# Two changes to an attention loop: the bursts of score products change places, and GpSimd takes over two small steps on the row maxima

## What is computed

```python
Q, K, V = heads(x @ Wq.T + bq), heads(x @ Wk.T + bk), heads(x @ Wv.T + bv)   # 32 query, 8 key/value heads of 16
Q, K = rope(Q, K)
w = softmax(Q @ K.T / 4)                        # per head 1024 x 1024, no mask
x = layernorm(x + (w @ V) @ Wo.T + bo)
x = layernorm(x + ffn(x))                       # silu(x Wg) * (x Wu) Wd, inner size 1408
```

## Time and profile before

| what | value |
|---|---|
| median of 3 runs | 1063.87 us (1063.75 to 1064.66) |
| profiled execution, its own time | 1064.13 us |
| its span, first to last instruction | 1062.3 us |
| PE busy | 97% |
| DVE busy | 76% |
| ACT busy | 63% |
| POOL busy | 25% |
| granted TensorE clock, mean | 0.998 of full speed |

### The profile page before, as it was taken

One profiled execution on the slowest core, in us unless ns is written; L12 is line 12 of the kernel. 1 busy time (PEld: TensorE's weight loads), 2 busy tenths in 40 slices (PEclk: granted clock), 3 DMA queues, 4 the chain that ended last, 5 costly groups with the idle time before them and its releaser, 6 DMA issues.

```text
span 1062.3 us, 15699 instructions
## 1 busy us (share of the span) xinstructions
PE 1026.5 (97%) x5858; PEld 536.8 (51%) x5858; DVE 809.5 (76%) x1199; ACT 665.1 (63%) x1346; POOL 266.2 (25%) x227
## 2 busy tenths in 40 slices
PE   8999999999999999999999999999999999999996
PEld 3643344433443433443444443333337888888885
DVE  4899978899779799779988899999803475662535
ACT  2368877788778788778766678888863431222221
POOL 2751030141335422246200042844100000000002
PEclk9999999999999999999999999999999999999999
DMA  5274417243142512344140446531217510402011
GB/s 200 80 196 126 106 35 213 52 97 78 52 115 75 105 56 54 82 108 105 34 78 12 116 120 150 124 121 37 93 68 193 166 40 9 111 28 52 1 39 42
DMA packets 64432, 94.87 MB, mean 89 GB/s; under 512 B 37536, under 2 KB 37920, under 8 KB 62272
## 3 DMA queue, kind: packets, MB, share of 16 engines
q1 hardware_dynamic: 63776, 93.10, 33.2%
q10 hardware_dynamic: 576, 0.72, 0.2%
HBM read 53.95 MB, written 27.00 MB: 76 GB/s over the span
## 4 chain that ended last, share of the span: by engine, by line
PE 80%; DVE 10%; ACT 6%; issue 2%; DMA 1%; SPq 0%; POOL 0%; DVEq 0%; POOLq 0%
PE PS L448 21%; PE PV L467 20%; PE PSA L537 15%; PE PS L554 5%; PE PSA L426 5%; DVE nmx L964 5%; PE PS L365 4%; ACT Bn L756 3%; PE PS L493 2%; PE PSA L493 2%; DVE nmx L960 2%; DVE nmx L957 2%; ACT Bn L765 2%; PE PV L554 2%; PE PSA L365 1%
## 5 line engine op out<-in xcount | busy, mean ns | idle before, releaser
L756 ACT ACTIVATE Bn<-PS 128x512 f32<-128x512 f32 x1146 | 548.8, 559 | 125.0 <-PE PS L448 111.1
L448 PE MATMUL PS<-Qt,Kt 50*128 50x512 f32 x1146 | 391.7, 434 | 20.0 <-ACT Bn L756 18.7
L426 PE MATMUL PSA<-Kt,Qt 48*128 48x512 f32 x1024 | 390.0, 459 | 2.2 <-DVE Kt L936 0.8
L964 DVE TENSOR_REDUCE nmx<-PSA 128x1 f32<-128x1024 f32 x256 | 312.2, 1219 | 61.0 <-PE PSA L426 59.8
L448 PEld LDWEIGHTS PS<-Qt,Kt 50*128 50x128 f32 x1146 | 184.4, 184 | 323.6 <-ACT Bn L756 312.7
L467 PE MATMUL PV<-Bn 128*32 128x512 f32 x2048 | 272.8, 605 | 0.0
L426 PEld LDWEIGHTS PSA<-Kt,Qt 48*128 48x128 f32 x1024 | 174.6, 183 | 21.7 <-DVE nmx L964 6.2
L960 DVE TENSOR_REDUCE nmx<-PSA 128x1 f32<-128x512 f32 x256 | 174.5, 682 | 1.4 <-PE PSA L426 1.1
L957 DVE TENSOR_REDUCE nmx<-PSA 128x1 f32<-128x512 f32 x256 | 174.3, 681 | 0.0
L537 PE MATMUL PSA<-x1Th,wr 128*128 128x512 f32 x344 | 135.0, 393 | 0.8 <-DVE sg L1052 0.5
L537 PE MATMUL PSA<-x1Tl,wr 128*128 128x512 f32 x344 | 134.7, 392 | 0.0
(11 more groups left out here) (166 smaller groups left out, 919.4 us busy)
## 6 DMA issues: line engine op xcount, KB each, us to landing
Qt<-pscr SPq DMA_DIRECT2D x90, 128.0 KB, 4.9
A<-in_wf SPq DMA_DIRECT2D x11, 768.0 KB, 6.3
wr<-A SPq DMA_DIRECT2D x33, 256.0 KB, 2.9
pscr<-A SPq DMA_DIRECT2D x16, 512.0 KB, 3.7
vscr<-Bn SPq DMA_DIRECT2D x32, 256.0 KB, 2.0
Kt<-pscr SPq DMA_DIRECT2D x90, 64.0 KB, 2.3
A<-A SPq DMA_DIRECT2D x16, 256.0 KB, 3.7
Bn<-vscr SPq DMA_DIRECT2D x8, 512.0 KB
```

The lines of the kernel that those rows point to most:

```text
L426: op = e.matmul(PSA[:, 2 * s + h, :], Qt[n % 3][p:p + NC_, g % 2, 128 * qt:128 * qt + 128], Kt[n % 3][p:p + NC_, 512 * h:512 * h + 512], s ...
L448: e.matmul(PS2[:, i, cols], Kt[n % 3][rows, 128 * kt:128 * kt + 128], Qt[n % 3][rows, g % 2, 512 * qh + cols.start:512 * qh + cols.stop], ...
L756: e.activation(Pb[c % NP_][:, cols], PS2[:, score_bank[c, p], cols], ACT.Exp, scale=0.25).then_inc(*act_exp.next(piece(c, p)))
L964: e.tensor_reduce(nmx[:, hh % 2, c0:c0 + 1], slot_pair(s), AX.XY, ALU.max, negate=True).then_inc(*dve_max[s].next(k))
```

## The change

- The weighing comes behind the fourth score tile in even units and behind the third in odd ones, so that the bursts of three and five change places; the tile in two pieces is now the one with c % 8 == 7, again the first behind the burst of three.
- Background work on PE stands right behind the weighing as before, which is now between the third and the fourth tile of the unit. ACT evacuates a projection there, and DVE does its adds and norms between the two parts of the unit's second step.
- For the half rows 1 to 30, DVE only joins the maxima in the unit with u % 8 == 3; POOL rounds and takes the rest; DVE transposes one unit later, behind its second step.
- SP calls `write_max` in the units with u % 8 == 4 (for the last half row in unit 243), still ahead of all else in that unit.
- Three steps of the rotation of the second projection come one unit later.

```diff
-                    (0, 4): (1, "rope"), (0, 7): (1, "h0"), (0, 9): (1, "h1"), (0, 10): (1, "out")}
+                    (0, 4): (1, "rope"), (0, 8): (1, "h0"), (0, 10): (1, "h1"), (0, 11): (1, "out")}
...
+        def apart(hh):
+            return 1 <= hh < 2 * NG - 1
+        def low_max(hh):
+            return (pool_ms if apart(hh) else dve_ms).at(("low", hh))
...
-            return [slice(0, 128), slice(128, 512)] if c % 8 == 3 and c < 4 * SPLIT else [slice(0, 512)]
+            return [slice(0, 128), slice(128, 512)] if c % 8 == 7 and c < 4 * SPLIT else [slice(0, 512)]
...
-            last = score_bank[4 * u + 3, len(pieces(4 * u + 3)) - 1]
+            last = score_bank[4 * u + 2, 0]
...
 # PE
-                    if u >= 1 and g == (2, 3)[u % 2]:
+                    if u >= 1 and g == (3, 2)[u % 2]:
                         weigh(u - 1)
+                        background(u)
...
 # ACT
                     exponent(u, g)
+                    if g == 2 and at_u in project_at:
+                        for h, i in enumerate(free_banks(u)):
+                            evacuate_raw(project_at[at_u], h, i)
...
 # DVE
-                if k % 16 == 15:
-                    turn_max(hh)
+                if 1 in halves and k % 16 == 15:
+                    join_max(hh)
+                    if not apart(hh):
+                        split_max(hh)
+                        turn_max(hh)
+                if 1 in halves and k % 16 == 1 and k > 16 and apart(k // 16 - 1):
+                    turn_max(k // 16 - 1)
...
+                k = next(steps)
+                if at_u in norm_at or at_u in out_at or at_u == values_at:
+                    maximum(k, (0,))
...
+                    maximum(k, (1,))
...
 # POOL
+            def split_max(hh):
+                top = nmx[:, hh % 2, 0:16]
+                w.wait_ge(*dve_ms.at(("join", hh)))
+                w.wait_ge(*dve_ms.at(("turn", hh - 1)))
+                e.tensor_copy(msp[:, 0:16], top).then_inc(*pool_ms.next(("high", hh)))
+                w.wait_ge(*pool_ms.at(("high", hh)))
+                e.tensor_tensor(msp[:, 16:32], top, msp[:, 0:16].bitcast(F32), ALU.subtract).then_inc(
+                    *pool_ms.next(("low", hh)))
...
+                if u % 8 == 3 and apart(steps_done(u) // 16 - 1):
+                    split_max(steps_done(u) // 16 - 1)
                 if at_u in project_at:
                     rope(project_at[at_u])
...
 # SP
-                if steps_done(u) // 16 > steps_done(u - 1) // 16:
+                if u % 8 == 4:
                     write_max(steps_done(u) // 16 - 1)
+                if u == SPLIT - 1:
+                    write_max(2 * NG - 1)
```

More of the change, by code:

```diff
@@ L251, in post_ln_layer @@
         dve_out, dve_turn, dve_parts = count("dve_out"), count("dve_turn"), count("dve_parts")
+        pool_ms = count("pool_ms")
         pool_one, pool_cs, pool_rope = count("pool_one"), count("pool_cs"), count("pool_rope")
@@ L665, in tensor, with background @@
                     project_half(1, 1, 3, ((0, 1), (2, 3))[k - 2])
+            def background(u):
+                at_u, pair = divmod(u, 16), free_banks(u)
+                if at_u in project_at:
+                    for h, i in enumerate(pair):
+                        project_half(project_at[at_u], h, i, (0, 1, 2, 3))
+                if at_u == values_at:
+                    for t in range(8):
+                        value_rows(1, t, pair[t // 4])
+                if at_u in out_at:
+                    t2 = out_at[at_u]
+                    out_project(False, 0, t2, [bank(i) for i in pair], [bank_free[i] for i in pair])
+                    for j, i in enumerate(pair):
+                        bank_free[i] = dve_y.at((False, 0, 2 * t2 + j))
             for u in range(SPLIT):
@@ L894, in scalar @@
                     exponent(u, g)
+                    if g == 2 and at_u in project_at:
+                        for h, i in enumerate(free_banks(u)):
+                            evacuate_raw(project_at[at_u], h, i)
                 if u >= 1:
                     finish(u - 1)
-                if at_u in project_at:
-                    for h, i in enumerate(free_banks(u)):
-                        evacuate_raw(project_at[at_u], h, i)
                 if at_u in rope_end and rope_end[at_u][1] in ("h0", "h1"):
@@ L945, in add_values, with maximum @@
                     ALU.add).then_inc(*dve_val.next((b, h)))
-            def maximum(k):
+            def maximum(k, halves=(0, 1)):
                 if k >= len(stream):
@@ L953, in maximum @@
                 if hh >= 2:
-                    w.wait_ge(*dve_ms.at(("low", hh - 2)))
+                    w.wait_ge(*low_max(hh - 2))
                 if by_halves(k):
[L956 to L961, removed]
+                    for h in halves:
+                        w.wait_ge(*pe_max.at((k, 0) if h == 0 else k))
+                        col = nmx[:, hh % 2, c0 + 16 * (h == 0):c0 + 16 * (h == 0) + 1]
+                        e.tensor_reduce(col, slot_pair(s)[:, h, :], AX.X, ALU.max, negate=True).then_inc(
+                            *dve_max[s].next((k, 0) if h == 0 else k))
                 else:
@@ L965, in maximum, with join_max @@
                         *dve_max[s].next(k))
-                if k % 16 == 15:
-                    turn_max(hh)
-            def turn_max(hh):
+                if 1 in halves and k % 16 == 15:
[5 more added lines that the diff above has]
+                    turn_max(k // 16 - 1)
+            def join_max(hh):
                 top, rest = nmx[:, hh % 2, 0:16], nmx[:, hh % 2, 16:24]
@@ L980, in turn_max @@
                     *dve_ms.next(("low", hh)))
-                w.wait_ge(*dve_ms.at(("low", hh)))
+            def turn_max(hh):
+                w.wait_ge(*low_max(hh))
                 if hh >= 2:
@@ L1218, in vector @@
                 maximum(next(steps))
[L1219 to L1226, removed]
+                k = next(steps)
+                if at_u in norm_at or at_u in out_at or at_u == values_at:
+                    maximum(k, (0,))
+                    if at_u in norm_at:
+                        first_norm(False, 0, norm_at[at_u])
+                    if at_u == values_at:
+                        for h, i in enumerate(free_banks(u)):
+                            add_values(1, h, i)
+                    if at_u in out_at:
+                        add_rows(False, 0, out_at[at_u], [bank(i) for i in free_banks(u)])
+                    maximum(k, (1,))
+                else:
+                    maximum(k)
                 if at_u in recip_at:
```

## The result

| | before | after |
|---|---|---|
| median of the runs | 1063.81 us | 1125.66 us (1123.25 to 1129.66, 4 runs) |
| ratio | | 1.0586, 95% interval 1.0574 to 1.0598 |
| profiled execution, its span | 1064.13, 1062.3 us | 1126.11, 1124.3 us |
| granted TensorE clock, mean | 0.998 | 0.962 |

The change makes the kernel 5.9% slower. Slower is what was forecast, but 1126 lies 7 us above the end of the range (1119).

What follows compares the result with a forecast made beforehand. The prediction took a ring of PE, ACT and DVE with little slack to bound the kernel. Its sum was 1064.1 - 19.2 (gains) + 60.7 (SP's order) + 2 (clock) = 1107.6 us, 1107 against the median; range 1078 to 1119.

Steps and rivals of the forecast that it cites:

- The copy (13.3): ACT's copy of PV moves behind the burst of five into idle time: 0.46 saved in 29 half rows, 13.3 us.
- the turn (5.9): Turn of the maxima split between DVE and POOL: PE's 0.44 stall goes in 14 half rows, 5.9 us gained.
- Background work and rounding at 0: Moved projection work on PE and ACT's rounding steps of the rotation: costs only change places, 0 us.
- The cover that I named for the rope: On POOL the rope waits behind the split, but its swap lands later anyway: 0 us.
- SP's order, 60.7: write_max on SP falls behind what u % 8 == 3 issues, so maxima land late at ten places: 60.7 us lost.
- t0: Start of PE's short piece in the unit with u % 8 == 3, from which SP's delays are counted.
- The two guesses at 512 KB and 768 KB in front: At (4,3) and (12,3) the gather runs behind big reads: 2.9 and 4.9 us lost.
- The clock, 2: PE's clock may fall behind the stalls; taken as 2 us, since most of a pair waits for ACT.
- The upper bound, 25: Clock term's upper bound: a pair at twice its time behind each of five stalls over 5 us, 25 us.
- The reciprocal's read does hold the write: Rival denied this: only gathers hold the maxima's write, (8,3) loses 8.2, losses 37.3, total 1082 us; chance 0.18.
- Small writes do not pass the big transfers: Rival said they pass: only SP's time to issue counts, 16.1 us lost, total 1061 us; chance 0.10.
- The gains did not fail: Rival said copy or POOL comes late each half row while stalls stay: up to 19 more, 1126 us; chance 0.06.

Runs made afterwards that it cites:

- the runs of each part alone: Kernel after with only the bursts, or only POOL's split of the turn, SP's order mended in both (the division moved too for the split): 1057.91 and 1061.37 us.
- the bursts alone: Kernel after with the whole turn back on DVE and SP's mended order (swap first, write_max ahead of reciprocal, parts and gather): 1057.91 us, ratio 0.9948.
- The version without stalls, the best version: Kernel after with write_max ahead of reciprocal, parts and gather, POOL's division moved to (12,12), input-column and weight loads moved: 1044.53 us, ratio 0.982.
- the first experiment: Kernel after with SP's write_max put back one unit earlier, in u % 8 == 3, ahead of all else: 1082.56 us, ratio 1.018.
- the old order of the bursts: Kernel before with only SP's write_max moved to u % 8 == 4, without the new bursts or POOL's part: 1151.55 us, ratio 1.0801.

## Why the prediction was right and wrong

- *The copy (13.3) and the turn (5.9).* Right. Quiet half rows went from 20.64 to 19.73, those with background work from 26.33 to 25.89; 14 x 0.91 + 15 x 0.45 = 19.5. The forecast priced each part by itself and added; the runs of each part alone show that this comes out only because both are made, since with the bursts alone the turn takes back most of the copy's gain where background work stands. The version without stalls measures 1044.5 where 1044.9 was worked out.
- *Background work and rounding at 0.* Right as long as the swap is on time: in the kernel after it was. The cover that I named for the rope ("its swap lands later anyway") holds only then; with the swap late, in the first experiment, the late rotations cost 28.6 with the low clock behind them.
- *SP's order, 60.7.* Right: 62.4 in the ten places named, each within 2.0. At (8,3) PE was foretold to be held to t0 + 23.6; the swap at t0 + 0.8 went out at 468.12, which makes 490.9, and PE went on at 491.11. The two guesses at 512 KB and 768 KB in front were low, 2.9 and 4.9 for 4.3 and 6.9; the others' errors nearly cancel.
- *The clock, 2 ("since most of a pair waits for ACT, I take 2").* **This step failed**, at 19.5. Two things were wrong in it. PE has hardly any slack within a pair even at 2.4 GHz: 4.72 of 4.94 busy in the window above, so at the low level the pair became PE's and took 6.2 to 8.3. The kernel before showed it as well, in a quiet half row of which PE was busy 20.04 us of 20.60 (columns as in the earlier trace rows):
```profile
104.30:124.90 20.60, 20.04 (x134) 7.68 (x132) 19.57 (x29) 17.48 (x37) 0.00 (x0) 1.00 0.46 98
```
An estimate from these rows: the pair at (3,0) began 0.37 ahead of the fall and had 4.72 of work; 0.37 at full clock and 6.83 at half do 3.8 of it, the other 0.9 comes at full clock, 8.1 in all; it took 7.9. And I counted the five waits over 5 us, while the clock fell around all ten, down to 1.6 us. The upper bound, 25, held in part by luck: it stands for five waits at 4.95 each, and there were ten, at 1.95 each on average. With it in the place of the value the sum is 1131; with the measured 19.5 it is 1125. The range's upper end "the clock upwards" should have reached there.
- *The rivals.* The reciprocal's read does hold the write: (8,3) lost 13.4, not 8.2, and (4,11) and (6,3) lost 3.1 and 3.6, not nothing. Small writes do not pass the big transfers: 10.17 us from issue to the read back. The gains did not fail (quiet half rows take 19.73); that the time of that rival, 1126, is the measured one is a coincidence.

## What to carry to other kernels

When a small transfer on which the bottleneck engine waits is moved one step later in a queue, all that was behind it is now ahead, and the time of its landing is set by their drain. Putting it back need not heal that: its own wait then holds the others, so sort the queue by what each needs before it can start and by who needs it next. And price a new stall of PE together with what comes behind it: a stretch at the low clock, in which PE is the engine without slack.

## What the runs showed of the hardware that I had not expected

- In the kernel after the clock fell to 1.2 GHz around all ten waits of 1.6 to 13.4 us. The long units behind them cost 1.2 to 3.0 us each, not in proportion to the wait (3.0 behind 1.6, 1.6 behind 13.4). In the old order of the bursts the same waits cost 29 instead of 19.5. The clock was low for longer there: around the longest wait its window is
```profile
490.80:511.20 20.40, 9.77 (x39) 3.69 (x39) 5.11 (x7) 5.94 (x13) 3.60 (x2) 0.50 0.29 48
```
where the kernel after has 13.65 us at 0.50 (482.48 to 496.13). Why it lasted longer no run tells. The shortest of the ten waits was 0.6 us there; the clock stayed at 1.00 (203 to 213), and no long unit follows.
- DVE's small steps waited for POOL: 0.17 alone; 1.20, 1.21 and 1.19 in one run, and 0.56 to 1.59 for seven joins in six other runs, every time ending 0.02 to 0.03 behind a POOL operation on 128x512 or 128x1024. The Trainium skill ("SBUF — State Buffer", Who interferes with whom) says that a DVE operation with two SBUF inputs and a POOL operation that reads SBUF lock each other out for a whole instruction; by that rule the trace agrees for the joins and the subtraction; for the rounding, with one input, no run here tells why. In the best version the join of one half row took 1.28, and the unit at (6,13), two behind it, 3.31 instead of 2.34.
- A product of 128 rows by 128 columns in float32 leaves two records and takes 0.229 us in a row of such.
